# A two-layer block on eight cores: DMA transposes of late tiles, norm sums over all chunks, and row-sum reciprocals through DRAM

## What is computed

```
xn = layernorm(x)
# layer 0
z  = sigmoid(xn Wz^T + bz);  h~ = xn Wh^T + bh
s  = scan over tokens of  (1 - z + 1e-8) * h_prev + z * h~
g  = silu( (silu(xn Wg^T) * (xn Wu^T)) Wd^T )        # weights are int / 127
x  = x + s * g
xn = layernorm(x)
# layer 1
q, k, v = xn Wqkv^T;  s = softmax(q k^T / 32) v      # 2048 x 2048, one head of 1024
xr, xk  = mixes of xn with the token before (mu_r, mu_k)
g  = silu( sigmoid(xr Wr^T) * (relu(xk Wk^T)^2 Wv^T) )
x  = x + s * g
```

## Time and profile before

| | us |
|---|---|
| three runs | 1173.62, 1174.21, 1264.25 (median 1174.21) |
| profiled execution | 1173.38 |
| its span, first to last instruction, slowest core | 1172.2 |
| spans of the eight cores | 1170.6 to 1172.2 |
| granted TensorE clock, every core | 1.000 |
| PE busy | 1152.0 (98%) |
| DVE / ACT / POOL busy | 551.2 / 259.5 / 131.0 |
| data moved by DMA | 124.82 MB, mean 106 GB/s |

### The profile page before, as it was taken

How to read it: one execution, slowest core, us unless ns; L and a number is a source line. 1 busy time by engine, 2 the same in 40 slices (tenths; PEclk the granted TensorE clock), 3 DMA queues, 4 the chain that set the end, 5 groups by cost and what they waited for, 6 DMA issues and landing times.

```text
span 1172.2 us, 15354 instructions; the slowest of 8 cores (1170.6 to 1172.2 us)
## 1 busy us (share of the span) xinstructions
PE 1152.0 (98%) x5480; PEld 529.7 (45%) x5480; DVE 551.2 (47%) x707; ACT 259.5 (22%) x323; POOL 131.0 (11%) x241
## 2 busy tenths in 40 slices
PE   4999999999999999999999999999999999999998
PEld 3444444444444444444444444444444444444444
DVE  5255111555656663225566884011134445555565
ACT  4222211122123111112212733533110110110110
POOL 3112111111111111111011122220000000000000
PEclk9999999999999999999999999999999999999999
DMA  9885844655664865545553589994000105355756
GB/s 214 208 138 96 193 74 71 106 110 100 110 114 69 164 129 74 81 88 97 112 107 55 89 123 154 159 149 117 1 18 19 37 19 115 77 125 114 137 122 176
DMA packets 88074, 124.82 MB, mean 106 GB/s; under 512 B 39744, under 2 KB 44096, under 8 KB 88000
## 3 DMA queue, kind: packets, MB, share of 16 engines
q0 software_dynamic: 31104, 65.03, 36.7%
q1 hardware_dynamic: 56896, 58.81, 20.0%
HBM read 159.47 MB, written 20.97 MB: 154 GB/s over the span
## 4 chain that ended last, share of the span: by engine, by line
PE 97%; DVE 1%; DMA 1%; ACT 1%; issue 0%; POOL 0%; SPq 0%; DVEq 0%; ACTq 0%; POOLq 0%
PE PS L156 96%; DMA S<-xtok 1%; PE PS L276 0%; ACT S L265 0%; DVE S L160 0%; DVE BN L242 0%; DVE BN L243 0%; DVE S L874 0%; POOL MV L253 0%; ACT S L286 0%; POOL S L127 0%; PE PS L843 0%; PE PS L842 0%; DVE MV L245 0%; DVE S L267 0%
## 5 line engine op out<-in xcount | busy, mean ns | idle before, releaser
L156 PE MATMUL PS<-S 128*128 128x512 bf16 x5264 | 1136.5, 378 | 2.3 <-DVE S L283 1.3
L156 PEld LDWEIGHTS PS<-S 128*128 128x128 bf16 x5264 | 513.8, 98 | 615.2 <-issue 3.7
L160 DVE TENSOR_TENSOR S<-S,PS 128x512 bf16<-128x512 bf16 x96 | 66.0, 688 | 183.6 <-PE PS L156 170.8
L369 ACT ACTIVATE S<-PS 128x512 bf16<-128x512 f32 x96 | 57.3, 597 | 244.5 <-PE PS L156 209.4
L814 ACT ACTIVATE S<-PS,CB 128x2048 bf16<-128x2048 f32 x16 | 31.5, 1967 | 225.0 <-DVE CB L812 206.0
L160 DVE TENSOR_TENSOR S<-S 128x512 f32<-128x512 f32 (+2 forms) x60 | 62.9, 1048 | 6.5 <-DVE S L532 0.3
L810 DVE TENSOR_REDUCE CB<-PS 128x1 f32<-128x1024 f32 x32 | 39.2, 1225 | 55.3 <-PE PS L843 33.4
L711 DVE SCALAR_TENSOR_TENSOR S<-S,PS 128x1024 f32<-128x1024 f32 x16 | 19.5, 1221 | 84.2 <-PE PS L156 83.9
L432 ACT ACTIVATE S<-PS 128x512 bf16<-128x512 f32 x32 | 19.1, 597 | 173.2 <-PE PS L156 173.2
L127 POOL DMA_DIRECT2D S<-wg x48 | 27.9, 581 | 257.3 <-PE PS L156 229.0
L761 DVE CAST S<-PS 128x512 bf16<-128x512 f32 x32 | 22.1, 692 | 47.2 <-PE PS L156 46.1
(11 more groups left out here) (73 smaller groups left out, 411.1 us busy)
## 6 DMA issues: line engine op xcount, KB each, us to landing
S<-wg POOLq DMA_DIRECT2D x48, 256.0 KB, 5.7
S<-wu POOLq DMA_DIRECT2D x48, 256.0 KB, 6.4
S<-wd POOLq DMA_DIRECT2D x16, 768.0 KB, 8.1
S<-xtok SPq DMA_DIRECT2D x16, 512.0 KB, 10.4
S<-xt SPq DMA_DIRECT2D x16, 512.0 KB, 16.0
x1s<-S SPq DMA_DIRECT2D x16, 512.0 KB, 3.2
S<-x1s SPq DMA_DIRECT2D x32, 256.0 KB, 5.7
out<-S SPq DMA_DIRECT2D x31, 256.0 KB, 3.8
```

The costliest lines, as they stand in the source:

```text
L156: ins = te.matmul(dst, l, r, start=(i == 0), stop=(i == n - 1))
L160: return DVE.did(ve.tensor_mul(o, a, b))
L369: at = ACT.did(se.activation(sil, ps(bg), AF.Silu, scale=1.0 / 127.0))
```

## The change

Three edits that do not touch each other:

1. `late0` is new: for each tile 8 to 15 two steps, statistics with 1/sigma, then the norm and `ln0_dma`, which SP issues as one DMA transpose of the tile straight into `XN`. There are 16 steps, where there were ten.
2. The norm sums of layer 1 run over all eight chunks. `stat_chunk(h, 7)` takes the place of `cast`; the split in high part and rest (`hilo`) follows there, first for the sum, then for the sum of squares. `sums` has two matmuls per group, the two groups of the sum first. The running sum moves to `TMP` at chunk 6 and `HILO` to the upper half of `TMP`.
3. `recip` makes only the reciprocal; POOL issues a DMA that writes the 128 numbers to the DRAM tensor `rs`, waits for it, and issues one that reads them back on all partitions. `spread(j)` stands right behind `recip(j)`; PE and DVE have no part in it. `av_scale` waits for the four reads of its quarter.

```diff
@@ -94,6 +94,7 @@
     identd = din("identd", [128, 128], BF16)
     out = nc.dram_tensor("out", [D, T], F32, kind="ExternalOutput").ap()
     x1s = nc.dram_tensor("x1s", [NC8, 128, T], F32, kind="Internal").ap()
+    rs = nc.dram_tensor("rs", [NT, 128], F32, kind="Internal").ap()
     gs = nc.dram_tensor("gs", [NC8, 128, T], BF16, kind="Internal").ap()
 
     es = contextlib.ExitStack()
@@ -103,7 +104,7 @@
     CB = es.enter_context(nc.sbuf_tensor("CB", [128, 64], F32))
     BN = es.enter_context(nc.sbuf_tensor("BN", [128, 16 * 12], F32))
     MV = es.enter_context(nc.sbuf_tensor("MV", [128, 64], F32))
-    DG = es.enter_context(nc.sbuf_tensor("DG", [128, 256], BF16))
+    DG = es.enter_context(nc.sbuf_tensor("DG", [128, 8], BF16))
     PS = es.enter_context(nc.psum_tensor("PS", [128, 4096], F32))
 
     def bf(col, n):
@@ -342,13 +343,18 @@
 
         early0 = [span1_a, span1_b, lambda: ln0_transpose(7, True), lambda: None]
 
+        x_sem = sems("s_xt", 4)
+
+        def ln0_dma(i):
+            SYN.after(ln0_tok[i])
+            dst = chunks(bf(XN + 8192, 8192), 8)[:, :, (i % 8) * 128:(i % 8 + 1) * 128]
+            xn_tok[i] = xnb_free[i % 4] = dma_t(dst, bf(XRK + (i % 4) * 1024, 1024), x_sem[i % 4])
+
+
         late0 = collections.deque()
-        for i in range(8, NT, 4):
-            late0.append(lambda i=i: [ln0_stats(q) for q in range(i, i + 4)])
-            late0.append(lambda i=i: (ln0_rstd(i, 4), [ln0_norm(q) for q in range(i, i + 4)]))
-            late0.append(lambda: None)
-            late0.append(lambda i=i: [ln0_transpose(q) for q in range(i, i + 2)])
-            late0.append(lambda i=i: [ln0_transpose(q) for q in range(i + 2, i + 4)])
+        for i in range(8, NT):
+            late0.append(lambda i=i: (ln0_stats(i), ln0_rstd(i)))
+            late0.append(lambda i=i: (ln0_norm(i), ln0_dma(i)))
 
 
         hs_free = collections.deque([None] * 4)
@@ -391,9 +397,9 @@
             x_tok[h, e] = dma(SYN, fp(X1 + e * 2048, 1024), xt[e * 128:(e + 1) * 128, h * HT:(h + 1) * HT], x1_sem[e])
 
 
-        acc_tok = {}
+        acc_tok, hl_tok = {}, {}
         sq_free = [None]
-        HILO = [TMP + i * 1024 for i in range(4)]
+        HILO = [TMP + 4096 + i * 1024 for i in range(4)]
 
         def stat_chunk(h, e):
             accx, accq, sq = fp(ACCX, 1024), fp(ACCQ, 1024), fp(SQ, 1024)
@@ -406,17 +412,28 @@
                 return
             t = ACT.did(se.activation(sq, xe, AF.Square))
             DVE.after()
-            DVE.did(ve.tensor_add(accx, fp(X1, 1024) if e == 1 else accx, xe))
+
+            src = fp(X1, 1024) if e == 1 else fp(TMP, 1024) if e == 7 else accx
+            accx = fp(TMP, 1024) if e >= 6 else accx
+            if e == 6:
+                DVE.after(mix_free[0])
+            ta = DVE.did(ve.tensor_add(accx, src, xe))
+            if e == 7:
+                DVE.after(ta)
+                hilo(0, accx)
             DVE.after(t, acc_tok[h])
             sq_free[0] = acc_tok[h] = DVE.did(ve.tensor_add(accq, accq, sq))
-            if e < 6:
-                return
-
-            for i, a in enumerate((accx, accq)):
-                DVE.after(mix_free[0])
-                t = DVE.did(ve.tensor_copy(bf(HILO[2 * i], 1024), a))
-                DVE.after(t)
-                acc_tok[h] = DVE.did(ve.tensor_sub(bf(HILO[2 * i + 1], 1024), a, bf(HILO[2 * i], 1024)))
+            if e == 7:
+                DVE.after(acc_tok[h])
+                acc_tok[h] = hilo(1, accq)
+
+        def hilo(i, a):
+
+            DVE.after(mix_free[1])
+            t = DVE.did(ve.tensor_copy(bf(HILO[2 * i], 1024), a))
+            DVE.after(t)
+            hl_tok[i] = DVE.did(ve.tensor_sub(bf(HILO[2 * i + 1], 1024), a, bf(HILO[2 * i], 1024)))
+            return hl_tok[i]
 
         def down_mix(h, e, kd, k):
             gslot = GG + (e % 2) * 1024
@@ -481,26 +498,15 @@
         def ln1_steps(h, xn_ready):
             XR, XK = XRH[h], XKH[h]
             st = {}
-            xb, sq = bf(SQ, 1024), bf(SQ + 1024, 1024)
             stats = [(fp(ST, 512), fp(ST + 1024, 512)), (fp(SQ, 512), fp(SQ + 1024, 512))]
 
-            def cast():
-                xe = fp(X1 + 7 * 2048, 1024)
-                DVE.after(x1_tok[h, 7], acc_tok[h])
-                st["xb"] = DVE.did(ve.tensor_copy(xb, xe))
-                ACT.after(x1_tok[h, 7], sq_free[0])
-                st["sq"] = ACT.did(se.activation(sq, xe, AF.Square))
-
             def sums():
-                for s in range(2):
-                    c = slice(s * 512, (s + 1) * 512)
-                    hl = [bf(o, 1024)[:, c] for o in HILO]
-                    PE.after(acc_tok[h], st["xb"])
-                    b = bank()
-                    st["mx", s] = (b, mms(ps(b), [(ones[:], r) for r in (hl[0], hl[1], xb[:, c])]))
-                    PE.after(st["sq"])
-                    b = bank()
-                    st["mq", s] = (b, mms(ps(b), [(ones[:], r) for r in (hl[2], hl[3], sq[:, c])]))
+                for i, key in enumerate(("mx", "mq")):
+                    PE.after(hl_tok[i])
+                    for s in range(2):
+                        b = bank()
+                        st[key, s] = (b, mms(ps(b), [(ones[:], bf(HILO[2 * i + k], 1024)[:, s * 512:(s + 1) * 512])
+                                                     for k in range(2)]))
 
             def stat():
                 tok = [None, None]
@@ -533,7 +539,7 @@
                 DVE.after(t, st["rstd"][s], xn_ready)
                 xn1_tok[h, s] = mul(dst, tq, rb)
 
-            steps = [lambda: None, cast, lambda: (sums(), stat())]
+            steps = [lambda: None, lambda: stat_chunk(h, 7), lambda: (sums(), stat())]
             for s in range(2):
                 for q in range(2):
                     steps.append(lambda q=q, s=s: affine(q, s))
@@ -779,9 +785,9 @@
         xc_sem, gc_sem, o_sem = sems("s_xc", 4), sems("s_gc", 4), sems("s_o", 4)
         xc_tok, gc_tok, o_tok = {}, {}, {}
         fin_free = [None] * 4
-        rb_tok = {}
+        rb_tok, rw_tok = {}, {}
+        rw_sem, rb_sem = sems("s_rw", 4), sems("s_rb", 4)
         rbuf_free = [None, None]
-        dg_free = [None]
 
         def fin_load(n):
             q, dc = n // 8, n % 8
@@ -821,30 +827,18 @@
             SYN.after(exp_tok[j], pt_free[q % 2], fold_pe)
             pt_tok[j] = pb_free[j % 4] = dma_t(dst, bf(PB + (j % 4) * 2048, 2048), pt_sem[j % 4])
 
-        dg_tok = {}
-
         def recip(j):
 
             q, i = j // 4, j % 4
-            DVE.after(exp_tok[j])
-            rc = CB[:, 42 + (j % 4):43 + (j % 4)]
-            t = DVE.did(ve.reciprocal(rc, mx(j, 3)))
-            DVE.after(t, dg_free[0])
-            t = DVE.did(ve.tensor_scalar(DG[:, 0:128], ident[:], rc, None, ALU.mult))
-            DVE.after(t)
-            dg_tok[j] = DVE.did(ve.scalar_tensor_tensor(DG[:, 128:256], ident[:], rc, DG[:, 0:128],
-                                                        ALU.mult, ALU.subtract))
+            DVE.after(exp_tok[j], rw_tok.get(j - 4))
+            rc = CB[:, 42 + i:43 + i]
+            POOL.after(DVE.did(ve.reciprocal(rc, mx(j, 3))))
+            rw_tok[j] = dma(POOL, rs[j].rearrange("(p o) -> p o", o=1), rc, rw_sem[i])
 
         def spread(j):
             q, i = j // 4, j % 4
-            b = bank()
-            PE.after(dg_tok[j])
-            te.matmul(PS[:, b * 512:b * 512 + 128], ones[:], DG[:, 0:128], start=True, stop=False)
-            mm = PE.did(te.matmul(PS[:, b * 512:b * 512 + 128], ones[:], DG[:, 128:256], start=False, stop=True))
-            dg_free[0] = mm
-            DVE.after(mm, rbuf_free[q % 2])
-            rb_tok[q] = DVE.did(ve.tensor_copy(fp(RB + (q % 2) * 1024 + i * 256, 128), PS[:, b * 512:b * 512 + 128]))
-            bank_free[b] = rb_tok[q]
+            POOL.after(rw_tok[j], rbuf_free[q % 2])
+            rb_tok[j] = dma(POOL, fp(RB + (q % 2) * 1024 + i * 256, 128), rs[j].partition_broadcast(128), rb_sem[i])
 
         def av_mms(q, dc, lo=0, hi=512):
             for tt in range(NT):
@@ -861,7 +855,7 @@
         def av_scale(q, dc):
 
             n = q * 8 + dc
-            DVE.after(rb_tok[q], gc_tok[n], o_tok.get(n - 4))
+            DVE.after(*[rb_tok[j] for j in range(4 * q, 4 * q + 4)], gc_tok[n], o_tok.get(n - 4))
             rbuf_free[q % 2] = mul(fp(OUTC[n % 4], 512), fp(RB + (q % 2) * 1024, 512), bf(GC + (n % 4) * 512, 512))
 
         def av_out(q, dc, b, mm, lo=0, hi=512):
@@ -890,8 +884,6 @@
             scores(j)
             if i:
                 p_transpose(j)
-            if j:
-                spread(j - 1)
             if q < 3:
                 y_unit(2 * i, q + 1)
                 y_unit(2 * i + 1, q + 1)
@@ -904,12 +896,12 @@
             if not i:
                 p_transpose(j)
             recip(j)
+            spread(j)
         while late:
             late.popleft()()
         bank_free[0:4] = s_free * 4
         ring.extend([0, 1, 2, 3])
         first = av_mms(3, 0)
-        spread(NT - 1)
         av_scale(3, 0)
```

## The result

The changed kernel takes 1255.81 us (median of 4 runs, 1252.64 to 1257.06) against 1174.06 (median of 3): a ratio of 1.0693, 95% interval 1.0679 to 1.0706. I had forecast 1169.9 with a range to 1173.5. All medians and single times from here on leave out executions in which the cores of a die ran visibly disturbed, in both kernels.

The account below looks back on a forecast made before the run. PE, busy 1152.0 of 1172.2 us, was taken as the bound. 7.05 us less work minus 3.25 of new waits gave 3.8 less than 1173.38, or 1169.6, set at 1169.9; range 1166 to 1173.5.

Parts of the forecast that it names:

- Sum of what goes from PE: PE loses transposes (3.56 us), spreads (1.76) and sum matmuls (1.73), together 7.05 us, with nothing added.
- the 3.56: Late tiles: 64 transposes leave PE, four groups of 16 at 0.89 us, giving 3.56 us.
- the 3 to 5 that I had named: Profile after: the eight DMA transposes of late tiles, on SP before the loads of x, land in 3 to 5 us.
- Waits at the norm sums: PE waits for DVE's additions and splits before layer 1's sums: 2.85 us in the second half, 0.4 in the first.
- rival 2: Waiting at the norm sums also lowers PE's clock to half, losing 2.5 us more; time 1172.1, chance 0.12.
- The way through DRAM: End of attention: write and read of reciprocals take 4 us each plus 0.55 per issue, 9.1 us, just in time.
- Rival 3: At the end, two DMAs of 14.0 us each bring the last row 20 us late for `av_scale(3, 0)`; 1182, chance 0.03.
- The other costs at nothing: DMA transposes, x loaded again, and work on DVE, ACT and POOL were taken as hidden, cost 0.
- x loaded again later: The eight loads go out 41 us later, but 45 us remain before first use against a landing of 16.0; hidden.
- the order on DVE and ACT: DVE's statistics come one tile at a time, ACT loses eight copies; PE waited for neither, cost 0.
- rival 4: Late DMA transposes hold up weight loads, making PE wait 1.5 us eight times, 12 us; time 1181.6, chance 0.03.

Follow-up runs that it names:

- e3: Kernel before with only the late tiles' transposes moved to DMA; 1170.78 us, ratio 0.9974.
- e15: Changed kernel with reciprocals written to DRAM as four runs of 128 bytes and the second half's norm sums 3.45 us later on PE; 1170.21 us, ratio 0.9960.
- e11: Changed kernel with reciprocals turned into rows by 32x32 transposes on DVE, so each write is four runs of 128 bytes; 1174.34 us, ratio 1.0008.
- Parts 1 and 2 together: Changed kernel with its third edit undone, so row sums go by diagonal matrices and PE as before; 1173.48 us, ratio 0.9998.
- e5: Changed kernel still writing the reciprocals to DRAM but reading a row of input x, so no read waits for a write (wrong scaling); 1235.28 us, one run.
- e12: Kernel before with only the norm sums over eight chunks, the second half's sums one output chunk later on PE; 1173.87 us, ratio 1.0005.

## Why the prediction was wrong

- **Sum of what goes from PE, 7.05 us: right.** 104 instructions are gone. Part 1 gave 3.0 (interval 1.9 to 4.3) of the 3.56. It costs no wait of PE, though its transposes land in 7.0 us in e3 and not in the 3 to 5 that I had named, on DMA engines busy with weights. e15, where all three gains stand, is 0.40% below before (2.9 to 6.5 us) and not 7 us; the wait of 0.3 us at the first sums, DMA waits of up to 1.5 at the start and a clock of 0.997 to 1.000 are in it.
- **Waits at the norm sums, 2.85 and 0.4: right.** Measured 2.94 and 0.33 us, at the instruction named (L435).
- **Clock behind that wait: left out of the sum, in it as rival 2.** Priced at 2.5 us with chance 0.12; it is real and of that size where it comes: 2.0 us behind the sums on e11's core 0, and 0.8 more in the sums themselves, but nothing on core 1. "TensorE: Matmul & The Clock Gate" of the Trainium skill, section "HAM oscillation — how this bites in real kernels", says that a long enough idle stretch sets the clock back. The trace agrees on most cores: 0.52 behind 2.63 us of waiting, and matmuls at full pace (0.22 us each) behind the waits of 1.3 and 0.9; three cores of the changed kernel and two of e11 keep 1.00 behind waits of the same length, which does not fit. Parts 1 and 2 together were to give 2.0 us and gave 0.2, with an interval of 1.3 either way.
- **The way through DRAM, "I take 4 each plus 0.55 for each issue, 9.1 us: just in time": this step failed.** The read is 3 to 4 us when nothing clogs. The write, taken at 4, is 6.8 to 15.0 at first and has a median of 20.6, and what it does to the other DMAs was not in the sum at all: that is 62 of the 79 us. I had no row for writes of 4 bytes side by side, bounded them by loads and stores of whole rows (1.9 to 9.0) and the 14.0 of a load, and picked by what was near in time, not in kind.
- **Rival 3 had the place and the direction**, at 1182 with chance 0.03. It missed twice. It charged only the end, though its own 29 us for the two DMAs are longer than any step (14 to 21), so that the delay must grow from step to step. And it took the write as latency of one DMA. e5 shows that 62 us come with no one waiting, since the other DMAs land late, above all the transposes of the probabilities.
- **The other costs at nothing held**: x loaded again later, the order on DVE and ACT, weights behind transposes (rival 4). e3 waits for none of them; its 1.6 us for weights lie near 26 and 54 us, ahead of the first late transpose, and e12, which has no part 1, waits 0.8 us for weights near 52 too.

## What to carry to other kernels

To spread one number per partition through DRAM, don't write 128 single words side by side: bring them together on a few partitions first (a 32x32 transpose makes four runs of 128 bytes), or leave 16 bytes and more between them. And price a new DMA twice, once for who waits for it and once for what it does to the DMAs beside it; the second can be read from the landing times of transfers that the change does not touch. A wait of PE of some 3 us can be worth more than its length (2.8 us more on one core here, nothing on another), and moving the waiting matmuls one unit of other work later is free where there is such work.

## What the runs showed that I had not expected

- 128 writes of 4 bytes into 512 consecutive bytes of DRAM land in 7 or 14 us, one core of each neighbouring pair in the one and the other in the other, though they take 0.1% of the DMA engines' time; in about half of that at 8 bytes from each other, in 1.7 to 2.7 at 16, in 1.7 on all cores at 64. In a kernel with 16 of them, other DMAs of the core land late: transposes in 19.5 us and not 4.3.
- In e12, two cores have a granted clock of 0.81 for 5 us, from 650 to 655, with PE busy all the time and no wait before; in e15 all four cores of one die have it from 650 to 660 (1.9 us lost on its slowest) and none of the other die. The profiled run of the kernel before shows 1.00 on all cores. What brings 0.81 stays open. The slowest core of e12:

```profile
649.00:650.00 1.00, 1.00 (x6) 0.41 (x5) 0.90 (x2) 0.91 (x2) 0.29 (x1) 0.97 1.06 160
650.00:651.00 1.00, 1.00 (x5) 0.43 (x4) 0.90 (x2) 0.54 (x1) 0.00 (x0) 0.81 0.86 88
```
